# Score banks three to two, maxima read in pairs, a ring for the strips' keys and values, half sums and gathering on GpSimd

## The chip, the cores and the metric

The kernel runs on one core of a Trainium2 chip. A core has TensorE (PE: matmuls, with PEld its weight loads), VectorE (DVE), ScalarE (ACT), GpSimd (POOL) and SyncE (SP), which here issues all DMAs. The metric is the device time of the one launch, in microseconds (us): setup, eight images, and the last store.

## The reference

Input x is (8, 128, 56, 56): eight images, 128 channels, 3136 tokens. Per image:

```
x = x + NeighbourhoodAttention(groupnorm(x))   # 16 heads of 8; each token sees its 7x7 window; softmax; proj
t = tokens(x)                                  # 3136 x 128
t = t + Attention(layernorm(t))                # 8 heads of 16, all 3136 tokens against all 3136
t = t + FFN(layernorm(t))                      # W @ dequantised NF4 weight
```

The second attention is by far the largest piece: 8 heads x 3136 x 3136 scores an image, and its softmax subtracts the true row maximum.

## The kernel before

**Two works side by side.** For each image there is a *front* (group norm, neighbourhood attention, second layer norm, the q, k, v of the second attention) and an *attention* (the second attention with its tail: projection, residual, layer norm, FFN). While image b is in attention, the front of image b+1 is woven in. The first image's front stands alone; the last image's attention has no front beside it.

**Attention.** An image has 14 units (`AUNITS`: two groups of four heads, seven blocks of 448 tokens). A unit has 25 chunks of 128 keys. In a chunk, for each of the four heads (`h`), TensorE makes a *score tile* 128x448 (`scores_turned`, L1026: four matmuls of 32 columns side by side) into one of `ST_BANKS` = 3 PSUM banks, and ScalarE reads it with the exponential into `PB` (L1242). Once a chunk TensorE *weighs* (`weigh`, L1041: the exponentials of the chunk before, times the values, fp32, eight records). The row maximum must be known before: while unit k is worked on, TensorE makes the scores of unit k+1 a first time as *maxima tiles* (`max_tile`, L962), 98 a unit, three or four a chunk, into three other banks, and VectorE reduces each to one column of `block_max` (`take_max`, L1469). TensorE waits for a bank before it writes it: for `exp_done` at a score tile, for `max_read` at a maxima tile. So the order in a chunk is

```
M0 ST0 [side slot 0] M1 ST1 M2 ST2 weigh [side slot 1] M3 ST3
```

**The side slots.** `Plan` is a table with a slot number t (the chunk, 350 an image) and a sub-slot 0 or 1. Every engine walks its own list of it in order of (t, sub). What TensorE puts in a side slot goes to the single PSUM bank `SIDE_BANK`, and the next one waits until the last was read. `fix` puts a task at a given slot, `place` at the next free one.

**The front's strips.** The neighbourhood attention goes by 28 strips of two rows, one every `PERIOD` = 9 chunks from chunk 39. A strip's window is 8 rows of keys and values (`WI`), cut into 14 units of 10 columns, 80 keys each. Strip s at t: three pieces of scores (TensorE L834; VectorE adds the bias table, L1331) at t to t+2, `maxima` (VectorE, L1340) t+3, `subtract` (GpSimd, L701) t+4, `exponentials` (ScalarE, L1119) t+5 in sub-slot 1, `sum_up` (VectorE, L1344) t+6, `invert_strip` and `normalise` (GpSimd, L706) t+8, four `turn`s (TensorE L843, ScalarE copies to `PT`, L1125) at t+12 to t+15, and `values` (TensorE L853; VectorE masks by head into `PVM`, L1354, and reduces to `On`, L1365) at t+17. Sub-slot 0 of t+7 is free. `Kn` holds the keys of the whole padded image; SyncE loads the eight value rows of each window anew (`load_windows`, L532).

**Setup.** SyncE fills the bias table `nat_bias` for five kinds of strip, eight DMAs each (L500); VectorE's first statistics (L1288) wait for it and for the padding of the value rows behind it.

## Time and profile before

| what | value |
|---|---|
| time, median of 3 runs | 9620.67 us (9618.12 to 9624.71) |
| the profiled execution: its own time | 9614.94 us |
| its span, first to last instruction | 9612.8 us |
| mean granted TensorE clock | 0.977 of full speed |

Busy time is that in which at least one instruction of the engine ran. A matmul's end is modelled: a tile of four matmuls is shown 0.36 us long where the next one starts 0.19 us later, so "busy" says that TensorE had work, not that it ran at its peak. "Idle before" is the engine's idle time just before the instructions of a row, with what ended it.

### The profile page before, as it was taken

How to read it: one execution, taken by the hardware profiler on the slowest of the kernel's cores; microseconds unless marked ns; L12 is line 12 of the kernel's file. 1: busy time of each engine (PE TensorE's matmuls, PEld its weight loads, DVE VectorE, ACT ScalarE, POOL GpSimd, SP SyncE). 2: the span in 40 equal slices, each digit the busy share in tenths (PEclk: the TensorE clock that was granted, in tenths of full speed). 3: DMA queues.
4: the chain of work that ended last, by engine and by line, in shares of the span. 5: the costliest groups of instructions: out<-in, count | busy, mean ns of one | idle time of the engine just before them, and what ended most of it. 6: DMA issues, size and time to landing. Idle time of an engine off the chain costs nothing.

```text
span 9612.8 us, 434952 instructions
## 1 busy us (share of the span) xinstructions
PE 8864.1 (92%) x173506; PEld 4432.8 (46%) x173506; DVE 7885.6 (82%) x14135; ACT 6505.8 (68%) x13345; POOL 1829.3 (19%) x1913
## 2 busy tenths in 40 slices
PE   4679999999999999999999999999999999999998
PEld 3434444444444444444444444444444444444543
DVE  4478888888888888888888888888888888889996
ACT  1247767767676666776767666676666766677777
POOL 4402221022211222112220122201222022210000
PEclk8779999999999999999999999999999999999999
DMA  2421221212112121121221112111121212111000
GB/s 57 67 52 29 38 39 34 48 33 37 36 32 49 34 38 32 49 35 33 39 39 43 33 35 41 36 47 34 33 37 36 54 27 36 38 39 31 8 10 8
DMA packets 516512, 354.32 MB, mean 37 GB/s; under 512 B 113245, under 2 KB 507213, under 8 KB 512461
## 3 DMA queue, kind: packets, MB, share of 16 engines
q1 hardware_dynamic: 514508, 325.98, 17.7%
q8 instruction: 1457, 23.87, 1.1%
q14 instruction: 547, 4.47, 0.2%
HBM read 233.15 MB, written 78.05 MB: 32 GB/s over the span
## 4 chain that ended last, share of the span: by engine, by line
PE 81%; issue 9%; DVE 6%; ACT 2%; POOL 1%; SPq 1%; DMA 0%; DVEq 0%; ACTq 0%; POOLq 0%
PE PS L962 22%; PE PS L1041 20%; PE PS L1026 19%; PE PS L792 6%; PE PS L834 6%; PE PS L843 4%; DVE block_max L1469 3%; PE PS L853 3%; ACT PB L1242 1%; DVE PVM L1354 1%; PE PS L816 0%; DVE SUMS L1344 0%; DVE X L1401 0%; POOL SC L701 0%; DVE X L1369 0%
## 5 line engine op out<-in xcount | busy, mean ns | idle before, releaser
L1242 ACT ACTIVATE PB<-PS 128x448 f32<-128x448 f32 (+1 forms) x11200 | 5464.7, 544 | 2195.1 <-PE PS L1026 2163.9
L1469 DVE TENSOR_REDUCE block_max<-PS 128x1 f32<-128x448 f32 x10878 | 6141.6, 616 | 760.5 <-PE PS L962 698.8
L962 PE MATMUL PS<-KP,QP 96*32 96x448 bf16 x43904 | 4177.7, 359 | 162.2 <-issue 54.9
L1026 PE MATMUL PS<-QP,KP 99*32 99x448 bf16 x43904 | 4195.9, 355 | 100.1 <-ACT PB L1242 54.6
L1041 PE MATMUL PS<-PB,VA 128*32 128x448 f32 x22400 | 2680.8, 543 | 14.2 <-issue 12.8
L962 PEld LDWEIGHTS PS<-KP,QP 96*32 96x32 bf16 x43904 | 1279.1, 96 | 1941.4 <-DVE block_max L1469 880.4
L1026 PEld LDWEIGHTS PS<-QP,KP 99*32 99x32 bf16 x43904 | 1298.0, 97 | 1288.5 <-issue 536.3
L1041 PEld LDWEIGHTS PS<-PB,VA 128*32 128x32 f32 x22400 | 731.3, 111 | 372.1 <-issue 43.4
L701 POOL TENSOR_TENSOR SC<-SC,NM 128x1120 f32<-128x1120 f32 x224 | 461.9, 2062 | 2055.8 <-DVE NM L1340 2055.8
L706 POOL TENSOR_TENSOR SC<-SC,SUMS 128x1120 f32<-128x1120 f32 x224 | 462.0, 2062 | 1999.9 <-DVE SUMS L1349 1999.9
L834 PE MATMUL PS<-Kn,QB 32*32 32x80 f32 x25088 | 623.5, 237 | 163.8 <-issue 92.4
L834 PEld LDWEIGHTS PS<-Kn,QB 32*32 32x32 f32 x25088 | 493.2, 108 | 423.8 <-issue 419.5
L1331 DVE TENSOR_TENSOR SC<-PS,nat_bias 128x80 f32<-128x80 f32 (+3 forms) x1120 | 394.9, 386 | 254.6 <-PE PS L834 235.8
L1125 ACT ACTIVATE PT<-PS 80x512 f32<-80x512 f32 (+1 forms) x896 | 480.3, 540 | 177.2 <-PE PS L843 173.7
L843 PE MATMUL PS<-C,SC 128*80 128x128 f32 x3136 | 503.9, 282 | 71.1 <-ACT SD L1136 15.4
L843 PEld LDWEIGHTS PS<-C,SC 128*80 128x80 f32 x3136 | 295.6, 120 | 383.4 <-issue 381.3
L728 POOL CAST shift_parts<-shift 14x128 bf16<-14x128 f32 x112 | 31.5, 281 | 2025.7 <-ACT shift L1155 2025.7
L853 PE MATMUL PS<-PT,VP 96*32 96x32 f32 x25088 | 283.0, 201 | 117.3 <-ACT PT L1125 59.0
L1344 DVE TENSOR_REDUCE SUMS<-SC 128x14 f32<-128x1120 f32 x224 | 293.9, 1312 | 100.0 <-ACT SC L1119 99.8
L853 PEld LDWEIGHTS PS<-PT,VP 96*32 96x32 f32 x25088 | 273.1, 113 | 166.3 <-issue 144.0
L742 POOL TENSOR_TENSOR normed<-tail 128x448 f32<-128x448 f32 x112 | 127.9, 1142 | 976.9 <-ACT tail L1164 976.9
L1340 DVE TENSOR_REDUCE NM<-SC 128x14 f32<-128x1120 f32 x224 | 293.4, 1310 | 0.8
(99 smaller groups left out, 3796.3 us busy)
## 6 DMA issues: line engine op xcount, KB each, us to landing
VP<-vT_padded SPq DMA_DIRECT2D x1792, 70.0 KB
QP<-q_dram SPq DMA_DIRECT2D x672, 56.0 KB, 2.1
k_dram<-k_parts SPq DMA_DIRECT2D x56, 336.0 KB, 4.9
q_dram<-q_parts SPq DMA_DIRECT2D x56, 336.0 KB, 2.7
KP<-k_dram SPq DMA_DIRECT2D x336, 56.0 KB, 2.2
KP<-k_dram SPq DMA_DIRECT2D x48, 392.0 KB, 5.9
VA<-v_dram SPq DMA_DIRECT2D x16, 816.0 KB, 4.4
vT_padded<-VTs SPq DMA_DIRECT2D x112, 112.0 KB
```

The lines of the kernel that those rows point to most:

```text
L701: G.tensor_tensor(SC[:, s % 2, :, :], SC[:, s % 2, :, :], m, ALU.add).then_inc(shifted, 1)
L706: G.tensor_tensor(SC[:, s % 2, :, :], SC[:, s % 2, :, :], r, ALU.mult).then_inc(normalised, 1)
L792: ins = mm(PS[at:at + 32, bank, 0:n], weights[:, at:at + 32], rhs, start=True, stop=True, tile_position=(0, at))
L834: ins = mm(PS[r, bank, (u - u0) * KEYS:(u - u0 + 1) * KEYS], QB[r, u, :], k_img[r, row:row + WI, u * QJ:u * QJ + WJ], start=True, stop=Tru ...
L843: ins = nc.tensor.transpose(PS[0:KEYS, bank, (u % 4) * P:(u % 4 + 1) * P], SC[:, s % 2, u, :], ident)
L853: ins = mm(PS[32 * g:32 * g + 32, bank, 32 * u:32 * u + 32], VP[0:KPAD, u, 32 * g:32 * g + 32], PT[0:KPAD, u, 32 * g:32 * g + 32], start=T ...
L962: ins = mm(PS[at:at + QT, bank, 0:BLK], QP[0:ROWS, Q_SLOTS[k % AUNITS], t:t + QT], KP[0:ROWS, g, t // BLK, j * BLK:(j + 1) * BLK], start=T ...
L1026: ins = mm(PS[k0:k0 + 32, bank, 0:BLK], KP[0:ROWSM, k // NBLK, h, c * P + k0:c * P + k0 + 32], QP[0:ROWSM, Q_SLOTS[k], h * BLK:(h + 1) * B ...
L1041: ins = mm(PS[32 * h:32 * h + 32, SUM_BANK, 0:BLK], VA[:, g, at:at + 32], exp_buffer(k, c)[:, h, :], start=(c == 0), stop=(c == CHUNKS - 1 ...
L1125: S.activation(PT[0:KEYS, u0:u1, :].rearrange("p u e -> p (u e)"), PS[0:KEYS, bank, 0:(u1 - u0) * P], ACT.Copy).then_inc(turned_read, 1)
L1242: S.activation(exp_buffer(k, c)[0:n, h, :], PS[0:n, at % ST_BANKS, 0:BLK], ACT.Exp, scale=float(ADIM) ** -0.5).then_inc(exp_done, 1)
L1469: V.tensor_reduce(block_max[:, q, j:j + 1], PS[:, bank, 0:BLK], AX.X, ALU.max).then_inc(max_read, 1)
```

## The change

- **Banks.** Score tiles have two banks instead of three, maxima tiles four instead of three. VectorE reads two maxima banks with one instruction; `max_read` then rises by two, and the first tile of a pair waits until the pair two before it is read.
- **Sum of a strip.** GpSimd first adds the two halves of the 80 exponentials (`halve_sum`, t+6); VectorE reduces 40 instead of 80, one slot later.
- **Values.** The mask is applied by ScalarE in four instructions (one a head of the four), the heads are added by GpSimd (`gather`, two instructions).
- **Ring.** Keys are made block by block (`k1` moves from chunks 25 to 31 to where `q1` is, and both three strips ahead), and GpSimd copies the new rows of each strip into an eight-row ring `KR` (`roll_keys`). The value rows are a ring too: a strip loads its new rows only, 56 an image instead of 224. Since rows wrap, the bias table has eight kinds of strip, and a piece that wraps needs two DMAs.
- `VTs` takes the place of part of `SC`.

```diff
@@ -33,7 +33,7 @@
 WIDE = SIDE + 2 * PADJ
 VROW = SIDE * 2
 MASKED = -1.0e30
-ROW_TYPES = [0, 1, 2, STRIPS - 2, STRIPS - 1]
+ROW_TYPES = [0, 1, 2, 3, 4, 5, STRIPS - 2, STRIPS - 1]
...
 AUNITS = GROUPS * NBLK
-ST_BANKS, MAX_BANK, MAX_BANKS, SUM_BANK, SIDE_BANK = 3, 3, 3, 6, 7
+ST_BANKS, MAX_BANK, MAX_BANKS, SUM_BANK, SIDE_BANK = 2, 2, 4, 6, 7
...
 SIDE_READER = {"gn_mean": "dve", "gn_var": "act", "k1": "dve", "v1": "act", "q1": "act", "scores": "dve",
-               "turn": "act", "values": "dve", "proj": "dve", "mean2": "dve", "var2": "act", "k2": "act",
+               "turn": "act", "values": "act", "proj": "dve", "mean2": "dve", "var2": "act", "k2": "act",
...
-            self.fix(t + 6, 0, "sum_up", s)
+            self.fix(t + 6, 0, "halve_sum", s)
+            self.fix(t + 7, 0, "sum_up", s)
+            self.fix(t + 2 * PERIOD - 1, 1, "gather", s)
...
             self.fix(t + 2 * PERIOD - 1, 0, "values", s)
+            self.fix(t - 5, 1, "roll_keys", s)
...
-            self.place(25 + j, "k1", j)
             t = self.place(25 + j, "v1", j)
...
         for j in range(NBLK):
-            t = FIRST_STRIP + PERIOD * BLOCK_STRIPS * j - 7
+            t = FIRST_STRIP + (PERIOD * (BLOCK_STRIPS * j - 3) if j else -7)
             self.fix(t, 1, "norm", NBLK + j)
-            self.place(t + 1, "q1", j)
+            t = self.place(t + 1, "k1", j)
+            self.place(t, "q1", j)
...
+def row_type(strip):
+
+    return strip if strip < 2 else 2 + (strip - 2) % 4 if strip < STRIPS - 2 else strip - STRIPS + len(ROW_TYPES)
+
+
+def ring_runs(rows):
+
+    runs = []
+    for row in rows:
+        if runs and row % WI == runs[-1][1] + runs[-1][2]:
+            runs[-1][2] += 1
+        else:
+            runs.append([row, row % WI, 1])
+    return runs
+
+
+def new_rows(strip):
+
+    row = window_row(strip)
+    return range(row if strip == 0 else max(row, window_row(strip - 1) + WI), row + WI)
+
+
+def windows_loaded(strip):
+
+    return sum(len(new_rows(n)) for n in range(strip % 2, strip + 1, 2))
+
...
-        Kn = sb("Kn", [P, SIDE * WIDE])
-        VTs = sb("VTs", [P, 4, P])
+        Kn = sb("Kn", [P, 2, BLK])
+        KR = sb("KR", [P, WI, WIDE])
         Qn = sb("Qn", [P, 2, BLK])
         QB = sb("QB", [P, UNITS, 32])
         SC = sb("SC", [P, 2, UNITS, KEYS])
+        VTs = SC[:, 1, :, :].rearrange("p u k -> p (u k)")[:, 0:4 * P].rearrange("p (c e) -> p c e", c=4)
+        HS = sb("HS", [P, UNITS, KEYS // 2])
...
-        PVM = sb("PVM", [P, BLK])
...
+            table_rows = 0
             for r, s in enumerate(ROW_TYPES):
                 for q in range(QI * QJ):
                     i = QI * s + q // QJ
                     at = first_key(i) - window_row(s)
                     ry = first_key(i) - i + KSZ - 1
-                    sp.dma_start(nat_bias[q:P:QI * QJ, r, :, at * WJ:(at + KSZ) * WJ],
-                                 stage1[q:P:QI * QJ, :, ry:ry + KSZ, :].rearrange("p t r k -> p t (r k)")
-                                 ).then_inc(table_rows_in, 16)
+                    for row, slot, n in ring_runs(range(window_row(s) + at, window_row(s) + at + KSZ)):
+                        y = ry + row - (window_row(s) + at)
+                        sp.dma_start(nat_bias[q:P:QI * QJ, r, :, slot * WJ:(slot + n) * WJ],
+                                     stage1[q:P:QI * QJ, :, y:y + n, :].rearrange("p t r k -> p t (r k)")
+                                     ).then_inc(table_rows_in, 16)
+                        table_rows += 1
...
-                    row = window_row(s)
-                    arrived(vT_out, of(b, ahead, 32 * NBLK, 32 * ((row + WI - 1) // BLOCK_ROWS + 1)))
+                    rows = new_rows(s)
+                    if len(rows) == 0:
+                        return
+                    arrived(vT_out, of(b, ahead, 32 * NBLK, 32 * ((rows[-1]) // BLOCK_ROWS + 1)))
                     arrived(pv_in, of(b, ahead, STRIPS, s))
-                    for ky in range(WI):
-                        src = bass.AP(tensor=vT_dram.tensor, offset=(row + ky) * (WIDE * P),
+                    for row in rows:
+                        src = bass.AP(tensor=vT_dram.tensor, offset=row * (WIDE * P),
                                       ap=[[P, WJ], [QJ * P, UNITS], [1, P]])
+                        ky = row % WI
                         sp.dma_start(VP[ky * WJ:(ky + 1) * WJ, :, :], src).then_inc(windows_in[s % 2], 16)
...
+                def roll_keys(s):
+                    rows = new_rows(s)
+                    if len(rows):
+                        pool.wait_ge(k1_read, of(b, ahead, NBLK, rows[-1] // BLOCK_ROWS + 1))
+                    wait(pool, scores_in, of(b, ahead, 3 * STRIPS, 3 * s))
+                    apart(pool)
+                    k_img = Kn.rearrange("p o (y x) -> p (o y) x", x=SIDE)
+                    runs = ring_runs(rows)
+                    if not runs:
+                        pool.sem_inc(keys_rolled, 1)
+                    for n, (row, slot, m) in enumerate(runs):
+                        ins = G.tensor_copy(KR[:, slot:slot + m, PADJ:PADJ + SIDE], k_img[:, row % (2 * WI):row % (2 * WI) + m, :])
+                        if n == len(runs) - 1:
+                            ins.then_inc(keys_rolled, 1)
...
+                def halve_sum(s):
+                    pool.wait_ge(exps, of(b, ahead, STRIPS, s + 1))
+                    wait(pool, summed, of(b, ahead, STRIPS, s))
+                    apart(pool)
+                    G.tensor_tensor(HS[:, :, :], SC[:, s % 2, :, 0:KEYS // 2], SC[:, s % 2, :, KEYS // 2:KEYS],
+                                    ALU.add).then_inc(sum_halved, 1)
+
+                def gather(s):
+                    j, at = s // BLOCK_STRIPS, s % BLOCK_STRIPS * (QI * SIDE)
+                    pool.wait_ge(masked, of(b, ahead, STRIPS, s + 1))
+                    if s % BLOCK_STRIPS == 0:
+                        wait(pool, proj_in, of(b, ahead, NBLK, j - 1))
+                        apart(pool)
+                    G.tensor_tensor(PVM[:, 0:2, :, :], PVM[:, 0:2, :, :], PVM[:, 2:4, :, :], ALU.add).then_inc(paired, 1)
+                    pool.wait_ge(paired, of(b, ahead, STRIPS, s + 1))
+                    v = PVM.rearrange("p h u (i j) -> p h i u j", i=QI)
+                    o = On[:, j % 2, at:at + QI * SIDE].rearrange("p (i u j) -> p i u j", i=QI, u=UNITS)
+                    G.tensor_tensor(o, v[:, 0, :, :, :], v[:, 1, :, :, :], ALU.add).then_inc(out_strip, 1)
...
-                    pe.wait_ge(xn_in, of(b, ahead, 2 * NBLK, j + 1))
-                    across(bank, W_qkv[:, P:2 * P], XN[:, j % 2, :]).then_inc(k1_in, 1)
+                    pe.wait_ge(xn_in, of(b, ahead, 2 * NBLK, NBLK + j + 1))
+                    across(bank, W_qkv[:, P:2 * P], XN[:, (NBLK + j) % 2, :]).then_inc(k1_in, 1)
...
-                    row = window_row(s)
                     pe.wait_ge(queries_in, of(b, ahead, STRIPS, s + 1))
-                    pe.wait_ge(k1_read, of(b, ahead, NBLK, (row + WI - 1) // BLOCK_ROWS + 1))
+                    pe.wait_ge(keys_rolled, of(b, ahead, STRIPS, s + 1))
...
-                lag = 0 if m == 0 and k % AUNITS == 0 else MAX_BANKS - 1
-                wait(pe, max_read, of(b, 0, AUNITS * MAXES, k * MAXES + m - lag))
+                wait(pe, max_read, of(b, 0, AUNITS * MAXES, k * MAXES + m + 1 - MAX_BANKS))
                 max_tile(k, m, max_bank(k, m))
...
                     bank = (k * (GH * CHUNKS) + at) % ST_BANKS
-                    seam = 1 if k == 0 and at < 2 else 0
-                    wait(pe, exp_done, of(b, 0, AUNITS * GH * CHUNKS, k * (GH * CHUNKS) + at + 1 - ST_BANKS + seam))
+                    wait(pe, exp_done, of(b, 0, AUNITS * GH * CHUNKS, k * (GH * CHUNKS) + at + 1 - ST_BANKS))
                     if n < P:
...
+                def values(s, bank):
+                    act.wait_ge(pv_in, of(b, ahead, STRIPS, s + 1))
+                    wait(act, out_strip, of(b, ahead, STRIPS, s))
+                    apart(act)
+                    pv = PS[:, bank, 0:BLK].rearrange("p (u h q) -> p h u q", u=UNITS, h=GH)
+                    for h in range(GH):
+                        ins = S.activation(PVM[:, h, :, :], pv[:, h, :, :], ACT.Copy, scale=head_mask[:, h:h + 1])
+                    ins.then_inc(masked, 1)
...
-                    wait(dve, scores_in, of(b, ahead, 3 * STRIPS, 0))
-                    V.tensor_copy(k_img[:, BLOCK_ROWS * j:BLOCK_ROWS * (j + 1), PADJ:PADJ + SIDE],
-                                  PS[:, bank, 0:BLK].rearrange("p (y x) -> p y x", x=SIDE)).then_inc(k1_read, 1)
+                    wait(dve, keys_rolled, of(b, ahead, STRIPS, max(4 * j - 5, 0)))
+                    V.tensor_copy(Kn[:, j % 2, :], PS[:, bank, 0:BLK]).then_inc(k1_read, 1)
...
-                    dve.wait_ge(exps, of(b, ahead, STRIPS, s + 1))
-                    V.tensor_reduce(SUMS[:, 0, 0:UNITS], SC[:, s % 2, :, :], AX.X, ALU.add).then_inc(summed, 1)
+                    dve.wait_ge(sum_halved, of(b, ahead, STRIPS, s + 1))
+                    V.tensor_reduce(SUMS[:, 0, 0:UNITS], HS[:, :, :], AX.X, ALU.add).then_inc(summed, 1)
...
-                def values(s, bank):
-                    dve.wait_ge(pv_in, of(b, ahead, STRIPS, s + 1))
-                    wait(dve, out_strip, of(b, ahead, STRIPS, s))
-                    V.tensor_tensor(PVM[:, :].rearrange("p (u h q) -> p u h q", u=UNITS, h=GH),
-                                    PS[:, bank, 0:BLK].rearrange("p (u h q) -> p u h q", u=UNITS, h=GH),
-                                    head_mask.rearrange("p (o h a) -> p o h a", o=1, a=1)
-                                    .to_broadcast([P, UNITS, GH, QI * QJ]), ALU.mult).then_inc(masked, 1)
-                    dve.wait_ge(masked, of(b, ahead, STRIPS, s + 1))
-                    j, at = s // BLOCK_STRIPS, s % BLOCK_STRIPS * (QI * SIDE)
-                    if s % BLOCK_STRIPS == 0:
-                        wait(dve, proj_in, of(b, ahead, NBLK, j - 1))
-                        apart(dve)
-                    v = PVM[:, :].rearrange("p (u h i j) -> p i u j h", u=UNITS, h=GH, i=QI)
-                    o = On[:, j % 2, at:at + QI * SIDE].rearrange("p (i u j) -> p i u j", i=QI, u=UNITS)
-                    V.tensor_reduce(o, v, AX.X, ALU.add).then_inc(out_strip, 1)
...
             def take_max(b, k, m):
+
+                if m % 2 == 0:
+                    return
                 dve.wait_ge(max_scores, of(b, 0, AUNITS * MAXES, k * MAXES + m + 1))
-                bank = MAX_BANK + (k % AUNITS * MAXES + m) % MAX_BANKS
-                q, j = max_step(m)
-                V.tensor_reduce(block_max[:, q, j:j + 1], PS[:, bank, 0:BLK], AX.X, ALU.max).then_inc(max_read, 1)
+                bank = MAX_BANK + (k % AUNITS * MAXES + m - 1) % MAX_BANKS
+                V.tensor_reduce(block_max.rearrange("p q j -> p (q j)")[:, m - 1:m + 1], PS[:, bank:bank + 2, 0:BLK],
+                                AX.X, ALU.max).then_inc(max_read, 2)
```

VectorE, amid strips (`NM`: the strip's maximum; `SUMS`: its sum and inverse; `block_max`: maxima tiles of attention). Before:

```order
L1340 TENSOR_REDUCE NM<-SC 128x14
L1469 TENSOR_REDUCE block_max<-PS 128x1 x12
L1344 TENSOR_REDUCE SUMS<-SC 128x14
L1469 TENSOR_REDUCE block_max<-PS 128x1 x8
L1354 TENSOR_TENSOR PVM<-PS,C 128x448
L1365 TENSOR_REDUCE On<-PVM 128x112
L1349 RECIPROCAL SUMS<-SUMS 128x14
L1469 TENSOR_REDUCE block_max<-PS 128x1 x2
```

Of the change:

```order
L1429 TENSOR_REDUCE NM<-SC 128x14
L1542 TENSOR_REDUCE block_max<-PS 128x2 x8
L1433 TENSOR_REDUCE SUMS<-HS 128x14
L1542 TENSOR_REDUCE block_max<-PS 128x2 x2
L1438 RECIPROCAL SUMS<-SUMS 128x14
L1542 TENSOR_REDUCE block_max<-PS 128x2 x2
```

Mask and gathering are gone from VectorE, the sum stands a chunk later, and every second take of a maximum is gone.

ScalarE, at a strip's values (`PB0`, `PB1`: the exponentials of attention; `PVM`: the masked values). Of the change; before, nothing stood between the exponentials there:

```order
L1333 ACTIVATE PB0<-PS 128x448 x4
L1333 ACTIVATE PB1<-PS 128x448
L1214 ACTIVATE PVM<-PS,C 128x112 x4
L1333 ACTIVATE PB1<-PS 128x448 x3
L1333 ACTIVATE PB0<-PS 128x448 x4
```

The four masking instructions stand behind the chunk's first exponential, and its other three behind them.

GpSimd, one strip (`KR`: the ring of keys; `QB`: spread queries; `HS`: half sums). Of the change; before, a strip had only `SC<-SC,NM`, `QB<-Qn,C` and `SC<-SC,SUMS`:

```order
L778 TENSOR_TENSOR SC<-SC,NM 128x1120
L739 COPY KR<-Kn 128x2x56
L753 TENSOR_TENSOR QB<-Qn,C 128x56x4 x2
L760 TENSOR_TENSOR HS<-SC 128x560
L769 TENSOR_TENSOR PVM<-PVM 128x224
L773 TENSOR_TENSOR On<-PVM 128x112
L783 TENSOR_TENSOR SC<-SC,SUMS 128x1120
```

Half sum and gathering stand between subtracting and normalising, and normalising waits behind them.

## Rows read from the trace of the kernel before

**Rows 1.** Engine totals of the page: busy us, share of the span, instructions.

```profile
PE 8864.1 (92%) x173506; PEld 4432.8 (46%) x173506; DVE 7885.6 (82%) x14135; ACT 6505.8 (68%) x13345; POOL 1829.3 (19%) x1913
```

**Rows 2.** Chain that ended last: of the page, then of 4190:5095 us.

```profile
PE 81%; issue 9%; DVE 6%; ACT 2%; POOL 1%; SPq 1%; DMA 0%; DVEq 0%; ACTq 0%; POOLq 0%
by line: PE PS L962 22.4%; PE PS L1041 19.5%; PE PS L1026 18.9%; issue 9.3%; PE PS L834 7.8%; PE PS L843 5.7%; PE PS L792 5.7%; PE PS L853 3.2%; DVE block_max L1469 2.7%; DVE PVM L1354 1.0%; DVE X L1369 0.5%; ACT PB L1242 0.4%; DVE VS L1387
```

**Rows 3.** Stretches: us; busy us (instructions) of PE, PEld, DVE, ACT, POOL; clock; DMA.

```profile
240.00:480.00 240.00, 152.97 (x4363) 113.40 (x4361) 118.09 (x192) 65.39 (x110) 110.07 (x95) 0.75 0.41 67
4190.00:5095.00 905.00, 855.86 (x17650) 423.07 (x17641) 764.98 (x1371) 627.24 (x1273) 208.83 (x212) 0.99 0.19 35
```

**Rows 4.** Stretches of line L1041 alone: us; busy us (instructions) of PE, PEld; clock; DMA.

```profile
4067.90:4108.10 40.20, 12.63 (x96) 3.07 (x96) 0.87 0.37 100
4189.70:5095.30 905.60, 249.15 (x2088) 66.19 (x2088) 0.99 0.19 35
8840.00:9590.00 750.00, 292.61 (x2464) 85.98 (x2464) 1.00 0.04 9
```

**Rows 5.** Timeline of one chunk: start, us, engine, line, op, count.

```profile
9264.19 0.93 PE L1041 MATMUL PS<-PB,VA 128*32 128x448 f32 x8
...
9264.95 0.36 PE L962 MATMUL PS<-KP,QP 96*32 96x448 bf16 x4
9265.14 0.36 PE L1026 MATMUL PS<-QP,KP 99*32 99x448 bf16 x4
...
9265.55 1.85 ACT L1242 ACTIVATE PB<-PS 128x448 f32<-128x448 f32 x4 [0.44 <-PE PS L1026]
...
9265.91 0.36 PE L1026 MATMUL PS<-QP,KP 99*32 99x448 bf16 x4
9266.10 0.36 PE L962 MATMUL PS<-KP,QP 96*32 96x448 bf16 x4
9266.29 0.36 PE L1026 MATMUL PS<-QP,KP 99*32 99x448 bf16 x4
9266.48 0.93 PE L1041 MATMUL PS<-PB,VA 128*32 128x448 f32 x8
```

**Rows 6.** Groups by line and shape: count | busy us, mean ns | idle before.

```profile
L1469 DVE TENSOR_REDUCE block_max<-PS 128x1 f32<-128x448 f32 x10878 | 6141.6, 616 | 760.5 <-PE PS L962 698.8
L1242 ACT ACTIVATE PB<-PS 128x448 f32<-128x448 f32 x10752 | 5256.8, 544 | 2096.9 <-PE PS L1026 2066.1 <-issue 2.3
...
L1344 DVE TENSOR_REDUCE SUMS<-SC 128x14 f32<-128x1120 f32 x224 | 293.9, 1312 | 100.0 <-ACT SC L1119 99.8
...
L1155 ACT ACTIVATE shift<-PS 14x128 f32<-14x128 f32 x112 | 29.9, 267 | 133.0 <-PE PS L909 132.5
L1480 DVE TENSOR_REDUCE block_max<-PS 128x2 f32<-128x896 f32 x28 | 29.1, 1078 | 38.7 <-PE PS L962 38.7
```

**Rows 7.** Timeline amid strips, behind the strip's exponential and at its sum.

```profile
4263.77 0.98 ACT L1242 ACTIVATE PB<-PS 128x448 f32<-128x448 f32 x2
4264.20 0.36 PE L1026 MATMUL PS<-QP,KP 99*32 99x448 bf16 x4
4264.28 1.31 DVE L1344 TENSOR_REDUCE SUMS<-SC 128x14 f32<-128x1120 f32 x1
...
4265.50 2.21 DVE L1469 TENSOR_REDUCE block_max<-PS 128x1 f32<-128x448 f32 x4
4266.17 0.10 PEld L962 LDWEIGHTS PS<-KP,QP 96*32 96x32 bf16 x4 [0.53 <-DVE block_max L1469]
```

**Rows 8.** Timeline amid strips, behind the matmuls with the values.

```profile
4272.21 2.06 POOL L706 TENSOR_TENSOR SC<-SC,SUMS 128x1120 f32<-128x1120 f32 x1 [12.38 <-DVE SUMS L1349]
4272.51 0.56 PE L1041 MATMUL PS<-PB,VA 128*32 128x448 f32 x1 [0.69 <-issue]
```

**Rows 9.** Timeline of setup: SyncE's table, VectorE's first statistics.

```profile
29.74 25.92 SPq L500 DMA_DIRECT2D nat_bias<-PB  x40
...
58.15 3.79 DVE L1288 BATCH_NORM_STATS2 stats<-X 128x6 f32<-128x448 f32 x7 [20.49 <-DMA vT_padded<-PB]
```

38 lines of the change are left out of this document (25 added, 13 removed).

## Prediction

> **What bounds the kernel now.** I read the views in this order: engine totals, chain of waits, stretches, then single instructions.
>
> The totals [rows 1] show TensorE busy 92% of the span, VectorE 82%, ScalarE 68%, GpSimd 19%. The chain [rows 2] agrees: 81% of the time that sets the end is on PE, 9% is "issue", 6% VectorE. So VectorE's total is not the bound; what counts is how long TensorE stands for it.
>
> The stretches tell two kinds of time apart. [Rows 4] count the weighing matmuls, eight records a chunk: in 8840:9590 (last image, attention alone) 2464/8 = 308 chunks in 750 us, in 4190:5095 (a middle image, attention beside the strips) 2088/8 = 261 in 905.6. A chunk takes 2.4 us where nothing or a tail stands beside it, and 3.5 with strips, and there PE is busy 855.86 of 905 us [rows 3].
>
> [Rows 5] show one bare chunk, weighing to weighing 9264.19 to 9266.48: 2.29 us. Eight tiles (L962 maxima, L1026 scores) follow at 0.19 us, then 0.75 us of weighing. No gap: this chunk is pure TensorE. But the others are close behind. A maxima read costs VectorE 6141.6/10878 = 0.565 us of busy time [rows 6], four of them 2.26; and ScalarE's four exponentials take 1.85 us from 9265.55, that is 0.41 us after the score tile of 9265.14, in steps of (1.85 - 0.544)/3 = 0.435 us [rows 5, 6].
>
> **The change, part by part.**
>
> *Maxima in pairs, four banks.* A single read takes 616 ns, a read of two banks 1078 [rows 6]: 154 ns less a pair, 5439 pairs, at most 838 us of VectorE. In bare chunks this buys nothing, since TensorE has no gap there. It also costs: a read starts when both tiles are in. The first tile of a pair waits for the pair two before it, so for M3 at 9264.95 in [rows 5] the read would start 0.41 later (taken from ScalarE's 0.41; an estimate for VectorE), end at 9266.44, and the tile of 9266.10 would start at about 9266.48. That wait exists only where a chunk begins on an even step, about half of them; on odd steps the weighing lies between.
>
> *Score banks, three to two.* Tile n+2 now waits for exponential n, where it waited for n-1. The score tiles of [rows 5] start at 9265.14, 0.38 later, 9265.91 and 9266.29. Exponential one ends at 9265.55 + 0.544 = 9266.09. A released tile starts about 0.04 us after its releaser (reads of L1469 end at 4265.50 + 0.616 = 4266.12, and PE loads at 4266.17 [rows 7]), so the third tile moves from 9265.91 to 9266.13: +0.22. Exponential two ends at 9265.55 + 0.435 + 0.544 = 9266.53, so the fourth starts at 9266.57 instead of 9266.51: +0.06. An odd chunk pays 0.28 us. On an even chunk the pair wait adds 9266.48 - 9266.32 = 0.16 and covers the 0.06: 0.38. Mean 0.33. Nothing later gives it back, because weighing and the next tile queue behind on TensorE, and the next chunk starts in the same state.
>
> It is paid where nothing stands in the chunk's first side slot (behind its first score tile); anything there of 0.28 us or more hides it. The plan has 350 such chunks in the last image and 104 in each of seven others, 25 of these amid strips: 350 + 7 x 79 = 903 outside. 903 x 0.33 = 298 us. I take 13 off, for the first 12 chunks of each middle image: [rows 4] have 40.2 us for 12, already 3.35 each. **+285.** Bounds: 0.2 a chunk (180) and 0.42 (380).
>
> *Strips: what VectorE gives back.* Per strip it loses the masking, the gathering, and half of the sum: 1312 ns becomes about 731, if 150 ns of it are fixed as in the reads of one bank and of two (2 x 616 - 1078 = 154) [rows 6]. What that is worth is read from TensorE's stalls: in 4190:5095 the chain gives 2.7% to block_max and 1.0% to PVM [rows 2], 33 us an image, 234 over seven. [Rows 7] show one such stall: the sum of 1.31 us at 4264.28, and behind it TensorE's load for L962, idle for 0.53 until a read is done. Much of the time behind the values is not VectorE's: in [rows 8] TensorE stands idle for 0.69 us on "issue" in the midst of the weighing. I take **-150**; bounds 0 and -234.
>
> *Strips: what is paid.* (a) The 25 free chunks an image there carry the score-bank wait too: 175 x 0.33 = +58. (b) The strip's exponential of 1.14 us sits on ScalarE between two of attention's: in [rows 7] the next one ends at 4263.77 + 0.544 = 4264.31, and the score tile of 4264.20, which did not need it, now does: +0.15 to 0.45, I take 0.3: 196 strips, +59. (c) The values are read by four ScalarE instructions of 128x112. None is shown; the nearest rows are 14x128 at 267 ns and 128x448 at 544 [rows 6], so 1.07 to 2.2 us for four. The row nearest in elements is the first; I take 1.1, mostly inside the time that values on TensorE and the "issue" break leave ScalarE: 0.1 a strip, +20; bounds 0 and +200 (1 us, nothing hidden). (d) GpSimd gets a half sum (560 elements, where 1120 take 2.06 us), two small adds and the key copy: under 2.06 us for the first and less for each other, some 3 us a strip. It stood idle for 12.38 us before it normalised [rows 8], and the turn that needs the result comes four chunks later. 0; bounds 0 and +1 us a strip (+196). (e) SyncE loads two rows a strip instead of eight; no tile is seen to wait for them in 4190:5095. 0; down to -60 if the code loads behind "issue" run shorter without them. Keys block by block move seven matmul groups within the plan: 0.
>
> *Setup.* The bias table takes 88 DMAs instead of 40, since rows wrap in the ring. 25.92/40 = 0.648 us each [rows 9], all on SyncE, and VectorE's first statistics start only behind them at 58.15. 48 x 0.648 = **+31**. Nothing covers it.
>
> In the part before attention each strip is a chain scores, maximum, subtract, exponential, turn, values, which neither the mask nor the half sum lengthens: 0, bounds -28 and +28 (1 us a strip).
>
> **Sum.** +285 - 150 + 58 + 59 + 20 + 31 = +303. The profiled execution took 9614.9 (span 9612.8): 9918. It stands 5.8 below the median of 9620.7, so 9924; I say **9920**.
>
> **The clock.** The granted clock is 1.00 in the last image and 0.99 amid strips [rows 4], idle gaps and all; it is 0.75, between its levels of 1.2 and 2.4 GHz, in 240:480, where PE is busy 152.97 of 240 us [rows 3]. The bare chunk would be busy 2.29 of 2.62 us, far nearer the first. The Trainium skill (TensorE: Matmul & The Clock Gate, HAM oscillation) says that idle gaps put the array back to its half clock. By that rule the score-bank waits would cost twice over; amid strips the trace speaks against it for gaps this short.
>
> **Rivals.**
> 1. *VectorE was the pacer after all, and the kernel gets faster.* For it: four maxima reads take as long as a bare chunk. Against it: TensorE has no gap in [rows 5]. It needs the bank wait under about 0.15 a chunk (135 + 26), because score tiles are released sooner than I reckon, and the whole 234 and the 60 of code loads gained: 161 - 294 + 31 = -102, 9519. The sign turns where 1078 chunks times the wait, plus 31, equals 294: at 0.24 us a chunk, with all else at its best.
> 2. *Both cancel.* Wait 0.2 (180 + 35), relief 234, the rest at nothing: +12, 9633.
> 3. *A milder loss.* Wait 0.25, relief 234, (b) and (c) halved: 226 + 44 - 234 + 40 + 31 = +107, 9728.
> 4. *GpSimd's and ScalarE's queues hold up the strips.* Each gather stands before normalise, each mask before an exponential: +1 us a strip on top, 9924 + 196 = 10120.
> 5. *The clock falls in bare chunks.* If half of the 903 ran at 1.2 GHz, 2.3 us more each: +1040, 10960. The 0.99 amid strips, where TensorE idles for 49 of 905 us, speaks against it.
>
> **How the numbers follow.** Forecast 0.62, rival 1 0.07, 2 0.04, 3 0.13, 4 0.12, 5 0.02. The forecast's own range, from 0.28 to 0.38 a chunk and relief -234 to -100, is 9800 to 10010. To leave out no more than 2 in 10 I reach half into rivals 3 and 4: 9740 to 10050. Faster by over 0.2% (what a measurement of this kernel can tell from none) 0.08, within 0.2% 0.03, slower 0.89.
>
> **What would show it.** In the bare stretches a chunk takes 2.55 to 2.7 us (PE's busy share falls less than that, since a tile is shown 0.36 long where the next starts 0.19 later), and score tiles wait for ScalarE's PB once or twice in each; the last image is 100 to 130 us longer. Amid strips hardly any tile waits for block_max behind a sum. The first statistics start at 89 us. VectorE's share falls to about 65%. I am wrong if bare chunks still take 2.3 us, or if amid strips more than 1 us a strip is gained.

## The result and the profile after

| kernel | time, median | range, runs | ratio to before, 95% interval |
|---|---|---|---|
| before | 9619.4 us | 9615.3 to 9624.7, 4 | |
| changed | 9967.7 us | 9956.9 to 9971.8, 4 | 1.036 [1.034, 1.038] |

The change makes the kernel 3.6% slower. The forecast was 9920, its range 9740 to 10050.

Engine totals, chain by engine and chain by line of the page, which answer to [rows 1, 2]. The second fence has the chain by line of the page before:

```profile
PE 9095.5 (91%) x173506; PEld 4227.4 (42%) x173506; DVE 7148.5 (72%) x8248; ACT 6856.4 (69%) x14241; POOL 2422.8 (24%) x2833
PE 78%; issue 8%; DVE 6%; ACT 6%; SPq 1%; DMA 1%; POOL 0%; DVEq 0%; ACTq 0%; POOLq 0%
PE PS L1119 20%; PE PS L1104 20%; PE PS L1042 19%; PE PS L875 6%; PE PS L914 6%; DVE block_max L1542 5%; ACT PB L1333 5%; PE PS L923 4%; PE PS L933 3%; SPq L538 1%; PE PS L961 1%; PE PS L897 0%; DMA vT_padded<-SC 0%; DVE X L1442 0%; DVE X L1474 0%
```
```profile
PE PS L962 22%; PE PS L1041 20%; PE PS L1026 19%; PE PS L792 6%; PE PS L834 6%; PE PS L843 4%; DVE block_max L1469 3%; PE PS L853 3%; ACT PB L1242 1%; DVE PVM L1354 1%; PE PS L816 0%; DVE SUMS L1344 0%; DVE X L1401 0%; POOL SC L701 0%; DVE X L1369 0%
```

VectorE has 737 us less to do and TensorE does the same work, yet ScalarE's share of the chain has gone from 2% to 6%. Of that, attention's exponentials (`PB`) have 5% for 1%: score tiles wait for their bank. VectorE keeps its 6% with less work, since `block_max` has gone from 3% to 5%. Windows of all engines, then of the weighing line alone, which answer to [rows 3, 4]:

```profile
240.00:480.00 240.00, 154.30 (x4410) 111.26 (x4410) 90.45 (x165) 85.82 (x181) 158.94 (x172) 0.78 0.13 35
4290.00:5195.00 905.00, 858.90 (x17474) 414.30 (x17470) 678.88 (x804) 647.05 (x1360) 278.72 (x320) 1.00 0.09 22
```
```profile
4321.00:5237.00 916.00, 248.60 (x2088) 65.93 (x2088) 1.00 0.08 21
9000.00:9750.00 750.00, 247.60 (x2120) 66.34 (x2120) 1.00 0.05 10
```

In the last image 2120/8 = 265 chunks take the 750 us in which 308 were done before; the granted clock is 1.00 there. Amid strips 261 chunks take 916 us for 905.6. One bare odd chunk, weighing to weighing 9476.78 to 9479.37, stands against [rows 5]:

```profile
9476.78 0.93 PE L1119 MATMUL PS<-PB,VA 128*32 128x448 f32 x8
...
9477.73 0.36 PE L1104 MATMUL PS<-QP,KP 99*32 99x448 bf16 x4
...
9478.11 0.36 PE L1104 MATMUL PS<-QP,KP 99*32 99x448 bf16 x4
...
9478.14 2.00 ACT L1333 ACTIVATE PB<-PS 128x448 f32<-128x448 f32 x4 [0.59 <-PE PS L1104]
...
9478.40 2.12 DVE L1542 TENSOR_REDUCE block_max<-PS 128x2 f32<-128x896 f32 x2 [0.48 <-PE PS L1042]
9478.74 0.10 PEld L1104 LDWEIGHTS PS<-QP,KP 99*32 99x32 bf16 x4 [0.52 <-ACT PB L1333]
...
9479.17 0.10 PEld L1104 LDWEIGHTS PS<-QP,KP 99*32 99x32 bf16 x4 [0.32 <-ACT PB L1333]
...
9479.37 0.93 PE L1119 MATMUL PS<-PB,VA 128*32 128x448 f32 x8
```

Score tiles start at 9477.73 and 9478.11; the next two wait for the exponential of two tiles back and start at 9478.74 and 9479.17, 1.01 and 1.06 us behind the starts of the tiles whose bank they take. The chunk takes 2.59 us for 2.29: +0.30, where 0.28 was forecast for an odd one. In the groups that answer to [rows 6] (count, busy us, mean ns, idle before):

```profile
L1542 DVE TENSOR_REDUCE block_max<-PS 128x2 f32<-128x896 f32 x5439 | 5848.1, 1088 | 1819.4 <-PE PS L1042 1777.3 <-issue 7.0
L1104 PEld LDWEIGHTS PS<-QP,KP 99*32 99x32 bf16 x43904 | 1244.5, 96 | 2159.4 <-ACT PB L1333 1267.3 <-issue 564.7 <-DMA QP<-shift_parts 4.5
L760 POOL TENSOR_TENSOR HS<-SC 128x560 f32<-128x560 f32 x224 | 311.4, 1390 | 830.5 <-ACT SC L1199 828.4
L769 POOL TENSOR_TENSOR PVM<-PVM 128x224 f32<-128x224 f32 x224 | 147.9, 660 | 1121.9 <-ACT PVM L1214 1121.9
L773 POOL TENSOR_TENSOR On<-PVM 128x112 f32<-128x112 f32 x224 | 94.1, 420 | 17.6
L1214 ACT ACTIVATE PVM<-PS,C 128x112 f32<-128x112 f32 x896 | 243.5, 354 | 208.3 <-PE PS L933 208.2
L1433 DVE TENSOR_REDUCE SUMS<-HS 128x14 f32<-128x560 f32 x224 | 163.1, 728 | 162.4 <-POOL HS L760 160.9
```

The start of the program, which answers to [rows 9]:

```profile
29.49 56.43 SPq L538 DMA_DIRECT2D nat_bias<-PB  x88
...
88.42 3.78 DVE L1377 BATCH_NORM_STATS2 stats<-X 128x6 f32<-128x448 f32 x7 [50.77 <-SPq L549]
```

**Where the time went.** Attention's exponentials, four a chunk, are a ruler: their starts cut every profiled run into the same stretches. The table has this for all kernels. The medians are of four runs, the stretches of the one profiled execution, which took 22 us more than the median in e3 and lay within 9 us of it elsewhere. So a difference of under 20 us between two rows can be the spread of single executions. "Bare" are chunks 309 to 350, with tails, "strips" chunks 39 to 309 and "first" 0 to 39, each summed over images 0 to 6; "start" is the time up to the first exponential.

| kernel | median | start | first | strips | bare | last image |
|---|---|---|---|---|---|---|
| before | 9619 | 587.0 | 828.0 | 6590.9 | 730.8 | 856.1 |
| changed | 9968 | 638.3 | 854.9 | 6611.1 | 849.4 | 990.5 |
| e1 banks put back | 9453 | 629.6 | 790.2 | 6417.1 | 731.4 | 856.8 |
| e2 before, banks alone | 10120 | 590.2 | 876.6 | 6797.4 | 852.6 | 990.5 |
| e3 single reads | 9830 | 636.9 | 826.0 | 6573.6 | 832.0 | 961.6 |
| e4 late table wait | 9946 | 626.0 | 852.1 | 6602.1 | 847.6 | 990.4 |
| e5 = e1, values on VectorE | 9514 | 625.1 | 792.1 | 6492.9 | 730.9 | 856.2 |
| e6 = e1, full sum | 9469 | 632.7 | 798.6 | 6438.0 | 729.1 | 856.4 |
| e7 = e1, eight rows | 9481 | 639.5 | 789.8 | 6444.0 | 732.4 | 856.8 |
| e8 = e1, setup | 9432 | 600.7 | 792.7 | 6424.9 | 730.1 | 856.4 |
| e9 weighing split | 10446 | 638.4 | 866.6 | 7075.0 | 857.6 | 990.2 |
| e10 split, single reads | 10360 | 633.3 | 851.9 | 7041.5 | 843.3 | 964.5 |
| e11 keys alone | 9535 | 623.0 | 790.4 | 6505.3 | 732.6 | 856.4 |
| e12 spaced tiles | 9975 | 635.1 | 808.3 | 6823.4 | 779.1 | 903.8 |

From before to changed: +51 before attention, +27 first, +20 strips, +119 bare, +134 last image: +351, of a span that grew by 352.

### The profile page after: what moved, and what is told of

Read it like the earlier page. It is cut to its first block, busy times and chain, and to the rows that moved or that the text cites. A ratio compares the mean times of both kernels' runs of the same rounds, so it can differ in the third digit from the quotient of the medians.

```text
span 9964.8 us, 431441 instructions
## 1 busy us (share of the span) xinstructions
PE 9095.5 (91%) x173506; PEld 4227.4 (42%) x173506; DVE 7148.5 (72%) x8248; ACT 6856.4 (69%) x14241; POOL 2422.8 (24%) x2833
## 4 chain that ended last, share of the span: by engine, by line
PE 78%; issue 8%; DVE 6%; ACT 6%; SPq 1%; DMA 1%; POOL 0%; DVEq 0%; ACTq 0%; POOLq 0%
PE PS L1119 20%; PE PS L1104 20%; PE PS L1042 19%; PE PS L875 6%; PE PS L914 6%; DVE block_max L1542 5%; ACT PB L1333 5%; PE PS L923 4%; PE PS L933 3%; SPq L538 1%; PE PS L961 1%; PE PS L897 0%; DMA vT_padded<-SC 0%; DVE X L1442 0%; DVE X L1474 0%
## 5 line engine op out<-in xcount | busy, mean ns | idle before, releaser
L1542 DVE TENSOR_REDUCE block_max<-PS 128x2 f32<-128x896 f32 x5439 | 5848.1, 1088 | 1819.4 <-PE PS L1042 1777.3
L1333 ACT ACTIVATE PB<-PS 128x448 f32<-128x448 f32 (+1 forms) x11200 | 5590.2, 543 | 2000.4 <-PE PS L1104 1907.3
L1104 PE MATMUL PS<-QP,KP 99*32 99x448 bf16 x43904 | 4163.6, 356 | 215.4 <-ACT PB L1333 135.9
L1042 PE MATMUL PS<-KP,QP 96*32 96x448 bf16 x43904 | 4122.5, 358 | 154.5 <-DVE block_max L1542 52.7
L1104 PEld LDWEIGHTS PS<-QP,KP 99*32 99x32 bf16 x43904 | 1244.5, 96 | 2159.4 <-ACT PB L1333 1267.3
L1042 PEld LDWEIGHTS PS<-KP,QP 96*32 96x32 bf16 x43904 | 1239.4, 96 | 1667.4 <-issue 682.0
L914 PE MATMUL PS<-KR,QB 32*32 32x80 f32 x25088 | 615.0, 236 | 105.7 <-DVE VS L1460 22.7
L914 PEld LDWEIGHTS PS<-KR,QB 32*32 32x32 f32 x25088 | 493.5, 108 | 343.8 <-issue 339.7
L760 POOL TENSOR_TENSOR HS<-SC 128x560 f32<-128x560 f32 x224 | 311.4, 1390 | 830.5 <-ACT SC L1199 828.4
L769 POOL TENSOR_TENSOR PVM<-PVM 128x224 f32<-128x224 f32 x224 | 147.9, 660 | 1121.9 <-ACT PVM L1214 1121.9
L1214 ACT ACTIVATE PVM<-PS,C 128x112 f32<-128x112 f32 x896 | 243.5, 354 | 208.3 <-PE PS L933 208.2
```

What stands on the lines that cost most here:

```text
L914: ins = mm(PS[r, bank, (u - u0) * KEYS:(u - u0 + 1) * KEYS], QB[r, u, :], KR[r, :, u * QJ:u * QJ + WJ], start=True, stop=True, tile_positi ...
L1042: ins = mm(PS[at:at + QT, bank, 0:BLK], QP[0:ROWS, Q_SLOTS[k % AUNITS], t:t + QT], KP[0:ROWS, g, t // BLK, j * BLK:(j + 1) * BLK], start=T ...
L1104: ins = mm(PS[k0:k0 + 32, bank, 0:BLK], KP[0:ROWSM, k // NBLK, h, c * P + k0:c * P + k0 + 32], QP[0:ROWSM, Q_SLOTS[k], h * BLK:(h + 1) * B ...
L1333: S.activation(exp_buffer(k, c)[0:n, h, :], PS[0:n, at % ST_BANKS, 0:BLK], ACT.Exp, scale=float(ADIM) ** -0.5).then_inc(exp_done, 1)
L1542: V.tensor_reduce(block_max.rearrange("p q j -> p (q j)")[:, m - 1:m + 1], PS[:, bank:bank + 2, 0:BLK], AX.X, ALU.max).then_inc(max_read, 2)
```

## Experiments

**The banks: put back, alone, and with single reads.** e1 and e2 differ from the changed kernel and from the one before by these lines (and the pair read with its waits):

```diff
-ST_BANKS, MAX_BANK, MAX_BANKS, SUM_BANK, SIDE_BANK = 2, 2, 4, 6, 7
+ST_BANKS, MAX_BANK, MAX_BANKS, SUM_BANK, SIDE_BANK = 3, 3, 3, 6, 7
```

> The changed kernel with its banks put back: three score banks, three maxima banks, every maxima tile read alone; strips, ring and setup stay as changed. Theory (the score-bank wait is the loss): bare chunks fall from 2.66 back to 2.29 us, which gives back the 280 us measured outside the strips, and amid strips the 200 us that TensorE idles for PB go too, less about 60 that the single reads cost again: 9968 - 280 - 140 = about 9550 us, 0.96 of the changed kernel and under the 9619 of the kernel before. Rival (the queues of GpSimd and ScalarE hold the strips up, and the waits for PB amid strips only stand in for them): only the 280 comes back, 9690 us, slower than the kernel before.

> The kernel before with the bank change alone: two score banks, four maxima banks read in pairs; strips, windows and setup as before. Theory: bare chunks take 2.62 to 2.66 us, +280 us outside the strips; amid strips the score-bank wait (+58 of free chunks, +59 behind the strip's exponential) against the relief that pairs give VectorE (half of the 234 or more): 0 to +60. Sum 9619 + 280 to 340 = 9900 to 9960 us. Rival (the strips' parts are the loss): well under +200, 9750 us.

e3 keeps two and four banks and reads each tile alone:

```diff
-                if m % 2 == 0:
-                    return
...
-                V.tensor_reduce(block_max.rearrange("p q j -> p (q j)")[:, m - 1:m + 1], PS[:, bank:bank + 2, 0:BLK],
-                                AX.X, ALU.max).then_inc(max_read, 2)
+                V.tensor_reduce(block_max[:, q, j:j + 1], PS[:, bank, 0:BLK], AX.X, ALU.max).then_inc(max_read, 1)
```

> The changed kernel with two score banks and four maxima banks, but each maxima tile read alone. It tells the pair wait from the score-bank wait. Theory (the score bank is the loss): even and odd bare chunks take the same 2.57 us, so outside the strips 0.1 x 450 = 45 us come back; amid strips VectorE has 154 ns a pair more to do and up to 80 us are lost: 9920 to 10000 us. Rival (the pair wait is most of the loss): bare chunks fall to 2.35 us or less and the time to about 9720.

Measured: e1 9453.1 us, 0.982 [0.980, 0.984] of before; e2 10120.4, 1.051 [1.049, 1.053]; e3 9829.5, 1.021 [1.019, 1.023]. Putting back the banks gives 515 us, adding them to the kernel before costs 494, so the bank change alone is more than the whole loss, and the rest of the change is a gain of 166 us. The rivals of e1 and e2 fall. My theory had the sign but missed by about 100 us in e1 and 160 in e2. Amid strips the banks cost 194 us (e1 to changed) and 206 (before to e2), where I had expected 140 and under 60. That is half of the miss in e1, whose other half is mostly 36 us outside the strips, and nearly all of it in e2. In e3 bare chunks stayed at 2.59 us, as the theory said and its rival did not, but the time fell 90 us below the theory's 9920: single reads cost nothing amid strips and gave back more than 45 us outside.

e3 splits the bank cost. In the last image, score banks cost (961.6 - 856.8)/350 = 0.30 us a chunk and pairs another 28.9/350 = 0.08, as [rows 5] gave them (0.28 and 0.05 on the mean). Amid strips two score banks with four maxima banks cost 157 us, and reading in pairs costs 37 more: it pays in no stretch. Over the whole launch the medians give the pairs 138 us and the score banks 376; the profiled executions give 115 and 404. Weight loads of the maxima (L962, L1042) and score tiles (L1026, L1104, L1106), amid strips of the middle image, before, changed, and e1, 905 us each; behind the second bar their idle time and what ended it:

```profile
L1026 PEld LDWEIGHTS PS<-QP,KP 99*32 99x32 bf16 x4088 | 117.4, 96 | 112.5 <-issue 55.9 <-ACT PB L1242 19.2
L962 PEld LDWEIGHTS PS<-KP,QP 96*32 96x32 bf16 x4092 | 115.4, 95 | 176.7 <-DVE block_max L1469 80.7 <-issue 53.0
```
```profile
L1104 PEld LDWEIGHTS PS<-QP,KP 99*32 99x32 bf16 x4040 | 114.9, 96 | 156.7 <-ACT PB L1333 74.3 <-issue 48.8
L1042 PEld LDWEIGHTS PS<-KP,QP 96*32 96x32 bf16 x4040 | 113.5, 95 | 143.9 <-issue 67.5 <-DVE block_max L1542 33.7
```
```profile
L1106 PEld LDWEIGHTS PS<-QP,KP 99*32 99x32 bf16 x4176 | 120.1, 97 | 114.9 <-issue 50.4 <-ACT PB L1335 23.0
L1042 PEld LDWEIGHTS PS<-KP,QP 96*32 96x32 bf16 x4180 | 118.3, 95 | 159.2 <-DVE block_max L1542 64.1 <-issue 48.5
```

These rows show the exchange, and not the loss itself: the change takes 47 us of the loads' idle time away from behind VectorE (80.7 to 33.7) and puts 55 behind ScalarE (19.2 to 74.3). e1 keeps 17 of the first and pays 4 of the second.

**The wait for the table, and two queues.** e4 moves VectorE's wait from ahead of the first statistics into the first bias add:

```diff
-            dve.wait_ge(table_complete, 1)
-            dve.wait_ge(vpad_out, 32)
...
+                    if s == 0 and p == 0 and ahead == 0:
+                        dve.wait_ge(table_complete, 1)
+                        dve.wait_ge(vpad_out, 32)
```

> The changed kernel, with VectorE's wait for the bias table and the value padding moved from ahead of the first statistics to ahead of the first strip's bias add. Theory (the +51 us before attention are mostly the table's DMAs on SyncE): statistics start at 38 us instead of 88, the first strip's maximum follows the table's end at 88 us by about 10 instead of 36, and the time falls by 25 to 30 us to about 9940. Rival (the value rows, whose stores wait on SyncE behind the table, hold the first strips up as well): the first values come no sooner and under 10 us are gained, 9960.

e8 does this on e1, and lets ScalarE's queue issue half the table:

```diff
-            for r, s in enumerate(ROW_TYPES):
+            for r, s in enumerate(ROW_TYPES[:4]):
...
+            act.wait_ge(stage_ready, 1)
+            for r, s in enumerate(ROW_TYPES):
+                if r < 4:
+                    continue
...
+                        act.dma_start(nat_bias[q:P:QI * QJ, r, :, slot * WJ:(slot + n) * WJ],
```

> The kernel with its banks put back (9453 us), with the bias table's DMAs halved between SyncE's and ScalarE's queues and the wait for it moved from the first statistics to the first bias add. Theory (in the run with the late wait alone the value stores still stood behind 88 DMAs on SyncE, and gained 12 us instead of 30): the table ends at about 59 us, value stores follow at once, the first strip's maximum comes at about 86 us instead of 124, and the time falls by 35 to 9418. Rival (DMA engines, not the queue, set the table's pace): it ends no earlier than 88 and the gain stays at 12, 9440.

Timelines, e4 first, then e8:

```profile
30.23 58.84 SPq L538 DMA_DIRECT2D nat_bias<-PB  x88
37.57 3.78 DVE L1375 BATCH_NORM_STATS2 stats<-X 128x6 f32<-128x448 f32 x7
...
91.68 19.36 SPq L563 DMA_DIRECT2D vT_padded<-SC  x14
94.12 0.60 ACT L1186 ACTIVATE SC<-PS 112x512 f32<-112x512 f32 x1 [46.57 <-DMA vT_padded<-SC]
```
```profile
29.78 28.91 ACTq L1182 DMA_DIRECT2D nat_bias<-PB  x44
29.82 28.52 SPq L539 DMA_DIRECT2D nat_bias<-PB  x44
37.57 3.78 DVE L1396 BATCH_NORM_STATS2 stats<-X 128x6 f32<-128x448 f32 x7
...
64.17 20.73 SPq L564 DMA_DIRECT2D vT_padded<-SC  x14
...
90.47 1.32 DVE L1451 TENSOR_REDUCE NM<-SC 128x14 f32<-128x1120 f32 x1
```

e4: 9946.5 us, 1.034 [1.031, 1.036]. The rival's mechanism held: statistics start 51 us sooner, but ScalarE's second block of value rows waits 46.57 us for a store that stands behind the table on SyncE, and attention starts 12 us sooner, not 25 to 30. The medians fall by 21 us, between the theory's 25 to 30 and the rival's "under 10"; e4's interval overlaps with that of the changed kernel, so the time alone decides nothing. e8: 9431.9 us, 0.981 [0.980, 0.983]. 44 DMAs take 28.9 us on one queue and 28.5 on the other at the same time, 0.65 us each as before, so the pace is each queue's. Attention starts 29 us sooner than in e1, and the time falls by 21 of the forecast 35. It is the fastest version run, though e1 lies within its interval.

**The strips' parts, each undone on e1.** Values (e5: mask and reduce on VectorE again), sum (e6: whole on VectorE, no half sum), and rows (e7: all eight loaded):

```diff
@@ e5: VectorE's values() as before; ScalarE's values() and gather() go @@
-               "turn": "act", "values": "act", "proj": "dve",
+               "turn": "act", "values": "dve", "proj": "dve",
@@ e6: halve_sum() goes, sum_up is at t + 6 again @@
-                    V.tensor_reduce(SUMS[:, 0, 0:UNITS], HS[:, :, :], AX.X, ALU.add).then_inc(summed, 1)
+                    V.tensor_reduce(SUMS[:, 0, 0:UNITS], SC[:, s % 2, :, :], AX.X, ALU.add).then_inc(summed, 1)
@@ e7 @@
-                    rows = new_rows(s)
+                    rows = range(window_row(s), window_row(s) + WI)
```

> The kernel with its banks put back (9453 us), and the strip's values again on VectorE: mask 0.62 us and reduce 0.99 us there, no four ScalarE instructions, no gathering on GpSimd. Theory (amid strips the 174 us that the parts other than the banks gained are VectorE's relief, shared by its length: 1.6 of 2.2 us): 0.73 x 174 = +125 us, about 9580. Rival A (the gain is SyncE's, two rows of value DMAs a strip for eight): under +20, 9460. Rival B (four ScalarE instructions and GpSimd's queue cost as much as VectorE gains): 9453 or less.

> The kernel with its banks put back (9453 us), and the strip's sum again whole on VectorE (1.31 us over 1120 elements for 0.73 over 560, no half sum on GpSimd), in the slot it had before. Theory (relief by length): 0.27 x 174 = +45 us amid strips, about 0 before attention: 9500. Rival (the relief is the DMAs', and the half sum's extra hop holds the strip's chain up): 9453 or less, with 10 to 20 us less before attention.

> The kernel with its banks put back (9453 us), but each strip loads all eight value rows of its window instead of the two new ones. Theory (VectorE's relief is the gain, DMAs run beside): within 15 us of 9453; TensorE's idle time on nothing but issue in the strips stays near that of the kernel it is made from. Rival (fewer DMAs shorten TensorE's code loads): the time rises by 60 to 110 us to about 9540, and the idle time on issue rises with it.

Measured: e5 9513.9 (0.990 [0.988, 0.991]), e6 9468.7 (0.985 [0.983, 0.986]), e7 9481.1 (0.986 [0.984, 0.988]); e1's interval is [0.980, 0.984]. Amid strips they cost 76, 21 and 27 us. Only the 76 of the values are clear of the spread: they are 60% of the 125 that VectorE's relief by length should have given. For the sum I had 45; it cost 21 by the profiled executions and 16 by the medians, and e6's interval overlaps with e1's, so that it is worth anything is not shown. e7 is 28 us slower than e1 by the medians. Of the 37 us by the profiled executions, 10 are before attention and 27 amid strips, where I had put under 15: the DMAs of the value rows are probably worth something, but how much is not settled.

e11 undoes all three, so that keys by block (with `q1` and its norm three strips ahead), their ring, the longer table and the new place of `VTs` are left:

> Old banks, values on VectorE, full sum on VectorE, all eight value rows loaded: what is left of the change is keys made block by block with the ring of keys, and the longer table. Undone one by one the parts cost 76 (values), 21 (sum) and 27 us (rows) amid strips, against 174 that all parts gained. Theory A (the rest, 50, and the 38 of chunks 0 to 39, are the keys'): strips take 6417 + 124 = 6541 us, chunks 0 to 39 790, and the time is 9453 + 124 = 9577. Theory B (the parts overlap in what they relieve, the keys give nothing amid strips): strips 6591, the time 9627.

Measured: 9534.9 us, 0.990 [0.989, 0.992]. Theory A stands, and put the gain of the keys too low (88 us, and the time at 9577): with the keys alone, strips fall from 6590.9 to 6505.3 and chunks 0 to 39 from 828.0 to 790.4. That is 123 us for an edit that I costed at nothing. Of the 38 in chunks 0 to 39, 30 are in chunks 25 to 31, from which `k1` moved away. Of the 86 amid strips nothing is in image 0 (921 us before, 929 in e11); each of images 1 to 6 gains 6 to 27. The three other parts together are worth 88 amid strips, where one by one they summed to 124. That may be since they relieve the same waits, but the 36 between are within the spread of three differences.

**Two tests of the spacing of tiles.** e9 cuts the weighing in two, to space score tiles evenly:

```diff
-                            if h == 2 and c > 0:
-                                weigh(k, c - 1)
+                            if h == 1 and c > 0:
+                                weigh(k, c - 1, range(0, 2))
+                            if h == 3 and c > 0:
+                                weigh(k, c - 1, range(2, 4))
```

> The changed kernel (9968 us; two score banks, four maxima banks, reads in pairs), with the weighing cut in two: heads 0 and 1 behind the chunk's second score tile, heads 2 and 3 behind its fourth, instead of all four behind the third. Same work, same banks; only the score tiles' spacing changes, from 0.38, 0.38, 0.38, 1.13 us to 0.38, 0.75, 0.38, 0.75. Theory (the bare chunk's loss is a tile that waits for the exponential of two tiles back, 0.41 + 0.544 + 0.04 = 1.0 us after that tile's start): two tiles back is now always 1.13 us, so nothing waits, the pair read's bank is free 1.9 us on, and a bare chunk takes 2.29 us again. Last image 857, -280 us outside the strips, and of the 171 us of waits for PB amid strips about half: 9968 - 280 - 85 = 9600 us. Rival (two banks are too few for ScalarE's throughput, or the pair read holds the chunk): bare chunks stay above 2.5 us and the time above 9850.

> The changed kernel with single reads from four maxima banks (9830 us), with the weighing cut in two as in the run beside it. Theory: bare chunks 2.29 us as well, since neither bank waits; it differs from the run with pairs only amid strips, where pairs spare VectorE 154 ns each (better for pairs) but were seen to cost 37 us as things stood (better for single reads). I expect both within 50 us: 9560 to 9640. Rival (the 4th maxima bank read alone is worth more than the third score bank): under 9453.

Measured: e9 10446.2 us (1.085 [1.083, 1.087]), e10 10359.6 (1.076 [1.074, 1.078]). The expectations failed by 850 and by over 700 us. Timeline of e9, matmuls of half a weighing:

```profile
9900.10 0.36 PE L1042 MATMUL PS<-KP,QP 96*32 96x448 bf16 x2
...
9900.12 0.54 PE L1119 MATMUL PS<-PB,VA 128*32 128x448 f32 x2
...
9900.29 0.35 PE L1104 MATMUL PS<-QP,KP 99*32 99x448 bf16 x2
...
9900.48 0.36 PE L1042 MATMUL PS<-KP,QP 96*32 96x448 bf16 x2
9900.50 0.54 PE L1119 MATMUL PS<-PB,VA 128*32 128x448 f32 x2
9900.88 0.36 PE L1042 MATMUL PS<-KP,QP 96*32 96x448 bf16 x2
```

A half is four records in two steps of 0.38 us, and the maxima tile goes on at 9900.88: 0.76 us in all, the same as for the whole of eight (9476.78 to 9477.54 in the changed kernel). The Trainium skill (TensorE: Matmul & The Clock Gate, the table's row on small-M matmuls) says that matmuls with outputs at different groups of 32 partitions run at once; the trace agrees: four heads together cost what two do. Meanwhile tiles of scores and maxima come by two matmuls instead of four (the rows with x2 at 9900.10, 9900.29 and 9900.48), so they start out of step. Two halves hold their groups for 1.5 us a chunk instead of 0.75, and a bare chunk takes 2.77 us for 2.59 (e9). In the last image the weight loads' idle time behind ScalarE's PB falls from 310 to 158 us, and the image takes 990.2 us as before the edit: weighing stands where waits had been. So the edit changed TensorE's work, and neither theory nor rival is decided by it.

e12 leaves the weighing whole and moves it (on e3):

```diff
-M0 ST0 [side slot 0] M1 ST1 M2 ST2 weigh [side slot 1] M3 ST3
+ST0 M0 [side slot 0] ST1 weigh [side slot 1] ST2 M1 ST3 M2 M3
```

> The kernel with two score banks and four maxima banks read one by one (9830 us), with the chunk's order changed and the weighing whole: ST0 M0, side slot 0, ST1, weigh, side slot 1, ST2 M1 ST3 M2 M3. In the run with the weighing cut in two, each half took as long as the whole (0.75 us, since the four heads' matmuls run side by side), so that the spacing of score tiles alone was not tried; here TensorE's work is untouched. Tiles two apart start 1.31, 1.31, 0.94 and 0.94 us after each other instead of 0.75 to 1.5, where 0.41 + 0.544 + 0.04 = 1.0 is needed. Theory (the loss is a matter of spacing): a bare chunk takes 2.29 + 0.05 to 0.1 us instead of 2.57; last image about 880 instead of 962, chunks 309 to 350 about 750 instead of 832, amid strips some 100 us back: 9830 - 82 - 82 - 20 - 100 = 9550 us. Rival (two banks can't carry four exponentials a chunk in any order, or side tasks beside the weighing cost more than is gained): bare chunks stay above 2.5 and the time above 9780.

Timeline of e12, one bare chunk, weighing 9502.38 to 9504.78:

```profile
9502.38 0.93 PE L1119 MATMUL PS<-PB,VA 128*32 128x448 f32 x8
...
9503.14 0.36 PE L1104 MATMUL PS<-QP,KP 99*32 99x448 bf16 x4
...
9503.52 0.36 PE L1104 MATMUL PS<-QP,KP 99*32 99x448 bf16 x4
...
9504.15 0.10 PEld L1104 LDWEIGHTS PS<-QP,KP 99*32 99x32 bf16 x4 [0.33 <-ACT PB L1333]
...
9504.58 0.10 PEld L1104 LDWEIGHTS PS<-QP,KP 99*32 99x32 bf16 x4 [0.31 <-ACT PB L1333]
...
9504.78 0.93 PE L1119 MATMUL PS<-PB,VA 128*32 128x448 f32 x8
```

The bare chunk takes 2.40 us with two score banks, next to the forecast of 2.34 to 2.39 and below the rival's 2.5, and the last image 903.8 (880 forecast) for 961.6. Spacing is most of the loss in bare chunks: 0.19 of 0.30 us. The rest stays: in the chunk shown two weight loads still stand idle behind PB, for 0.33 and 0.31 us. But the kernel takes 9975.5 us, 1.036 [1.034, 1.038], since amid strips 250 us are lost instead of 100 won: here the rival's other half held, that side tasks beside the weighing cost more than is gained. Chunks with nothing in side slot 0 gain 186 us over e3, in and outside the strips; the other chunks of the strips take 292 us more. Over all strips the idle time of TensorE's matmuls behind ScalarE's PB rises from 61 us in e3 to 297. Why that order is so bad there was not tried further.

## Why the prediction was right, and where it wasn't

The forecast was 48 us low. Its sign, its mechanism (the score tile waits for the exponential of two tiles back) and its main term hold; that the sum came so near is in part luck, since misses of 190 us up and 143 down stand in it. Point by point:

- **Score banks and pairs, +285 in bare chunks.** The difference of changed and e1 outside strips is 64.7 + 118.0 + 133.7 = 316 us. Of it 307 are in the 840 chunks with a free first side slot that the plan has in these stretches: 0.36 a chunk for 0.33. (The prediction counted 903, with 25 an image amid strips; up to chunk 309 the plan has 34 there, so some 20 us of its term belong amid strips.) Seen alone, before to changed gives 280, but that contains -38 from the keys: the nearness of 280 to 285 is partly luck.
- **Strips, -13.** Measured +20, from far larger parts: the banks +194, keys by block -86, the rest -88. I had +117 for the bank wait ((a) and (b)), 0 for the keys, and -150 for VectorE's relief, pairs included, which the runs show to cost 37 there. Of the banks' 194, 83 are in 238 free chunks (0.35 each, as outside) and 111 in the 1652 others, where I had 59 for the strip's exponential and took anything of 0.28 us in the side slot to hide the wait: it does not hide all of it.
- **Pairs relieve VectorE by 154 ns each.** This term was mis-sized. Busy time of the reads fell from 6141.6 to 5848.1: 293 us, 54 ns a pair, not up to 838. The 616 ns are the mean length of one record; in a row reads follow each other every 0.53 us ([rows 7]: four in 2.21, so (2.21 - 0.616)/3), and 6141.6/10878 = 0.565 was the price. The Trainium skill (Perfetto Trace Analysis, Optimizing Scalar/DVE Operations) says of the access overhead of such an instruction that the profiled one is about twice the engine's busy time, since the write-acknowledgement half overlaps with the next instruction. The trace agrees that records overlap, by 0.616 - 0.53 = 0.09 us. So the pairs had little to pay for a wait of their own with, and VectorE's share is 72%, not the 65 forecast.
- **(c) four masks on ScalarE:** 4 in 1.09 us, 1.1 forecast. **Half sum:** 728 ns on VectorE for 731; 1.39 us on GpSimd, under its bound. Rival 4 is refuted: with these queues and the old banks the kernel is faster (e1, e5, e6).
- **(e) fewer DMAs, 0, down to -60:** e7 gives -27, not well clear of the spread. **Keys, 0:** -123, the step that failed most. I counted seven moved matmul groups and did not ask what they leave behind in chunks 0 to 39 (-38), nor what the strips gain. The idle time of TensorE's matmuls amid strips that is put down to "issue" (gaps of over 0.15 us, images 0 to 6) is 175 us before and 196 in e2, which has the old keys too; it is 75 in e11 with the same eight rows loaded, and 62 to 88 in changed, e1, e5, e6 and e7. Image 0, whose strips gained nothing, has 11 us of it before and 13 in e11; the other six have 19 to 34 each before and 7 to 12 after. So these breaks go with the keys and are as large as the 86; why they shorten stays open.
- **Setup, +31:** first statistics at 88.42 for 58.15, +30.3. Attention starts another 21 later: some 6 with keys alone (e11), 7 more with the other parts and 9 with the banks. Kernels with two score banks that are alike up to there (changed, e3, e9, e10, e12) start between 633.3 and 638.4, so each of these is hardly above the spread, and their causes are not shown. I had 0, with bounds of -28 and +28.
- **Rival 5, the clock:** the granted clock is 1.00 (2.4 GHz) in both stretches, with 0.30 us of waits in the bare chunk shown. Waits this short did not cost the clock, so the rule that the prediction weighed does not reach them. Rivals 1 to 3 need a bank wait of 0.25 a chunk or less; it is 0.36.
- **The tally.** Against the sum of +303 the profiled runs show +351. The terms were off by: banks outside strips +31, banks amid strips +77, VectorE's relief, sum and rows -88 for -150, which is +62, (c) -20 (it lies in the -88), keys -123, the part before attention +20. Together +47: the misses are larger than their sum, and the keys, which I had at nothing, hid most of the rest.

## What to carry to other kernels

Count a PSUM bank by the distance from a tile's start to its release against the distance at which its bank is asked for again: here three score banks hid 1.0 us and two did not. By the medians 376 us hung on that and 138 on reading in pairs, while all that was done for VectorE and the DMAs amid strips was worth 88. Price an instruction that stands in a row by busy time over count, not by its mean length. A bundle of edits should be taken apart before it is judged: this one was 166 us of gain under 515 of loss, and e1, with the banks put back, is 1.8% faster than the kernel before.

## What the runs showed of the hardware

- Weighing for four heads, on four groups of 32 output partitions, takes 0.76 us, and so it does for two heads (e9).
- Two issuing engines fill a table of small DMAs twice as fast as one: 88 in 56.4 us on one queue, 44 and 44 in 28.9 (e8).
- GpSimd adds 112 elements a partition in 0.42 us, 224 in 0.66 and 560 in 1.39: by these three, an estimate of 0.18 us and 2.2 ns an element. Its subtraction over 1120, another form, takes 2.06 us, less than twice the add of 560.
- VectorE's reads of one bank are 0.616 us long in the profile and follow each other every 0.53 us; a read of two banks costs 1.075 us of busy time for 1.13 of two single reads.
- TensorE's breaks with no releaser shown depend on what else the program places about: 175 us amid strips before, 75 in e11, with the same value rows loaded.
- The granted clock stays at 1.00 where a bare chunk of 2.59 us has 0.30 us of waits (changed, last image).
